# Adjacency attention on one core: three units of seven products in a pass from the sixth pass on, a new order of tiles, the shared product in a unit's second step, left sums in two parts

## What is computed

```python
h = maximum(layernorm(x), 0)                     # x is 4096 x 512
q = h @ Wq.T + bq;  k = key @ Wk.T + bk;  v = value @ Wv.T + bv
scores = (q @ k.T) / 64 * adj                    # adj is 4096 x 4096, of zeros and ones
scores = where(abs(scores) < 1e-5, -1e9, scores)
out = x + (softmax(scores) @ v) @ Wm.T + bm
```

## Time and profile before

| | |
|---|---|
| median of 3 runs | 1549.62 us (1547.48 to 1549.89) |
| the profiled execution | 1546.85 us, its span 1545.0 us |
| TensorE busy | 1522.7 us, 99%, 7064 matmuls |
| VectorE, ScalarE, GpSimd busy | 1061.2, 633.7, 217.9 us |
| DMA, mean share of 16 engines | 73%, 283 MB |

### The profile page before, as it was taken

The page is one execution under the profiler, slowest core; times in us unless marked ns, Lnnn a source line. Parts: engine busy times, 40 slices in busy tenths (PEclk is TensorE's granted clock), DMA queues, the critical chain, the costliest instruction groups (busy, mean ns, idle before and its releaser), DMA issues.

```text
span 1545.0 us, 23780 instructions
## 1 busy us (share of the span) xinstructions
PE 1522.7 (99%) x7064; PEld 700.5 (45%) x7064; DVE 1061.2 (69%) x2191; ACT 633.7 (41%) x1040; POOL 217.9 (14%) x291
## 2 busy tenths in 40 slices
PE   8998999999999999999999999999999999999998
PEld 5543444444444444444444444444444444444444
DVE  5989777766667666666766666676666767676662
ACT  5776433434343333334333334343333434333332
POOL 6164000020020101002010010201001020200100
PEclk9999999999999999999999999999999999999999
DMA  9834786678868687686868768676866868787664
GB/s 346 280 78 98 184 200 154 155 194 217 200 164 205 150 229 173 168 209 157 206 155 231 173 162 210 154 211 163 223 171 162 212 149 216 170 211 174 147 163 109
DMA packets 459508, 283.24 MB, mean 183 GB/s; under 512 B 377411, under 2 KB 385859, under 8 KB 459334
## 3 DMA queue, kind: packets, MB, share of 16 engines
q1 hardware_dynamic: 459456, 282.67, 72.7%
q10 hardware_dynamic: 6, 0.01, 0.0%
HBM read 175.38 MB, written 15.73 MB: 124 GB/s over the span
## 4 chain that ended last, share of the span: by engine, by line
PE 92%; DVE 3%; ACT 2%; DMA 2%; issue 1%; SPq 0%; ACTq 0%; DVEq 0%
PE R L833 15%; PE R L835 15%; PE R L834 15%; PE S L833 11%; PE S L835 11%; PE S L834 11%; PE M L833 3%; PE M L835 3%; PE M L834 3%; PE R L951 1%; PE R L904 1%; DMA pT<-ph 0%; DMA Kbuf<-key_factors 0%; DVE Vbuf L1581 0%; DMA pT<-osb 0%
## 5 line engine op out<-in xcount | busy, mean ns | idle before, releaser
L1293 ACT ACTIVATE drop<-Zbuf 128x512 f32<-128x512 f32 x256 | 161.1, 629 | 687.9 <-DVE cmx L1605 557.7
L833 PE MATMUL R<-Vbuf,pT 128*128 128x512 f16 x1008 | 382.1, 379 | 4.8 <-DMA pT<-ph 2.4
L835 PE MATMUL R<-Vbuf,pT 128*128 128x512 f16 x1008 | 382.0, 379 | 0.0
L834 PE MATMUL R<-Vbuf,pT 128*128 128x512 f16 x1008 | 382.0, 379 | 0.0
L833 PE MATMUL S<-Kbuf,qT 128*128 128x512 f16 x738 | 279.7, 379 | 0.0
L834 PE MATMUL S<-Kbuf,qT 128*128 128x512 f16 x738 | 279.7, 379 | 0.0
L835 PE MATMUL S<-Kbuf,qT 128*128 128x512 f16 x738 | 279.7, 379 | 0.0
L1657 DVE SCALAR_TENSOR_TENSOR Zbuf<-S,rs,adjb 128x512 f32<-128x512 f32 x178 | 133.5, 750 | 210.2 <-PE S L835 199.8
L1605 DVE CUSTOM_DVE_ANT_0 Zbuf<-drop,Zbuf 128x512 f32<-128x512 f32 x256 | 178.2, 696 | 0.0
L833 PEld LDWEIGHTS R<-Vbuf,pT 128*128 128x128 f16 x1008 | 98.6, 98 | 125.8 <-DMA pT<-ph 4.9
L835 PEld LDWEIGHTS R<-Vbuf,pT 128*128 128x128 f16 x1008 | 98.6, 98 | 118.9
(11 more groups left out here) (277 smaller groups left out, 1828.7 us busy)
## 6 DMA issues: line engine op xcount, KB each, us to landing
Kbuf<-key_factors SPq DMA_DIRECT2D x134, 512.0 KB, 4.2
adjb<-in_adj_dram SPq DMA_DIRECT2D x256, 256.0 KB, 2.9
xq<-in_x_dram SPq DMA_DIRECT2D x32, 256.0 KB, 2.8
Kbuf<-in_L_gnn_key_dram SPq DMA_DIRECT2D x8, 1024.0 KB, 13.7
xr<-in_x_dram SPq DMA_DIRECT2D x32, 256.0 KB, 3.0
out_dram<-xr SPq DMA_DIRECT2D x31, 256.0 KB, 4.3
Vbuf<-in_L_gnn_value_dram SPq DMA_DIRECT2D x7, 1024.0 KB, 7.9
key_factors<-early SPq DMA_DIRECT2D x32, 128.0 KB, 2.3
```

The costliest lines, as they stand in the source:

```text
L833: nc.tensor.matmul(ps, lhs[0], rhs[0], start=start, stop=False, skip_group_check=added)
L834: nc.tensor.matmul(ps, lhs[0], rhs[1], start=False, stop=False, skip_group_check=added)
L835: return nc.tensor.matmul(ps, lhs[1], rhs[0], start=False, stop=stop, skip_group_check=added)
L1293: nc.scalar.activation(drop[:, :], tile_of(s.i, s.j), ACT.Abs).then_inc(abs_ready, 1)
```

## The change

From the sixth pass on a third unit is made of tiles 3 and 2, at steps 2 and 3, ahead of the other two; its second half is in steps 9 and 11, so that steps 8 to 12 and 14 all have six score matmuls. The fourth and fifth pass keep two units. The order of tiles is new in all passes after the first, in both halves and for the probabilities. T2 moves from a unit's step 0 to its step 1, ahead of T1, and the sum of it on VectorE with it. The left sums are made in two parts: GpSimd begins in step 0 instead of step 1 and hands over S1 and S2 first, ScalarE copies two halves of 512 columns, and VectorE makes the low half of the first at the end of step 2, of the second in step 3 behind `tile_max`. Four more factors stay in `Kbuf`, in the place of key tiles 2 and 3 (slots -4 to -1); a pass has 13 factor loads in place of 10. The factors' sums are made in the bank `M0`, and 16 more half-pieces are made in steps 3 of the fourth to 2 of the fifth pass. Six passes are now written out. `kept` is renamed `common`.

```diff
-        UNITS = [(5, 4), (7, 6)]
+        UNITS = [(5, 4), (7, 6), (3, 2)]
...
             return Vbuf[:, :].bitcast(fp16)[:, at:at + D]

-        FIRST_ORDER, SECOND_ORDER = [0, 1, 2, 3, 5, 4, 7, 6], [4, 0, 5, 1, 6, 2, 7, 3]
-        SECOND_PROBS = [4, 5, 6, 7, 0, 1, 2, 3]
-        UNIT, NU, MAKE_STEP, FIRST = 4, len(UNITS), 19, 4
+        FIRST_ORDER, SECOND_ORDER = [0, 1, 3, 2, 5, 4, 7, 6], [4, 2, 5, 3, 6, 0, 7, 1]
+        SECOND_PROBS = [3, 2, 5, 4, 7, 6, 0, 1]
+        UNIT, NU, MAKE_STEP, FIRST = 4, len(UNITS), 19, 6
+        TWO_FROM, THREE_FROM = 3, 5
         RING_Q, MIX_Q = (4, 5, 6), 7
+        KEPT_TWO = {(0, "B11"): 0, (0, "T2"): 1, (1, "B11"): 2, (1, "T2"): 3}
+        KEPT_THREE = {(2, "B11"): -4, (2, "T2"): -3, (0, "B21"): -2, (1, "B21"): -1}
+        TURNS_TWO = {4: [(0, "B21"), (1, "B21"), (0, "T3"), (1, "T4")], 5: [(0, "T1"), (1, "T1"), (0, "T4")],
+                     6: [(0, "B22"), (1, "B22"), (1, "T3")]}
+        TURNS_THREE = {4: [(2, "B21"), (0, "T1"), (1, "B22"), (0, "T4"), (1, "T4")], 5: [(2, "T1"), (0, "B22"), (0, "T3"), (2, "T4")],
+                       6: [(2, "B22"), (1, "T1"), (2, "T3"), (1, "T3")]}
...
-        XF = W[0]
+        XF = M0
+        LATE = [W[0], S[0], S[1]]
...
+                if s.three:
+                    if s.j == 3:
+                        sp.wait_ge(kt_stored, 16 * 2 * len(PIECES))
+                        wait(sp, scores_done, s.t)
+                        load_factor((0, "T1"), 4)
+                        wait(sp, unit_mm, 3 * s.before + 3)
+                        load_factor((0, "B22"), 5)
+                    if s.j == 4:
+                        wait(sp, scores_done, s.t)
+                        load_factor((1, "T1"), 6)
+                    if s.j == 5:
+                        wait(sp, unit_mm, 3 * s.before + 6)
+                        load_factor((1, "B22"), 4)
+                    if s.j == 6:
+                        wait(sp, scores_done, s.t)
+                        load_factor((0, "T3"), 5)
+                    if s.j == 7:
+                        wait(sp, unit_mm, 3 * s.before + 9)
+                        load_factor((2, "T3"), 6)
+                    if s.j in (8, 9, 10, 11):
+                        wait(sp, scores_done, s.t)
+                        load_factor(((0, "T4"), (2, "T4"), (1, "T3"), (1, "T4"))[s.j - 8], (4, 5, 6, 4)[s.j - 8])
+                    if s.prefetch and s.j in (12, 13, 15):
+                        wait(sp, scores_done, s.t)
+                        load_factor((2, {12: "T1", 13: "B22", 15: "B21"}[s.j]), {12: 5, 13: 6, 15: 4}[s.j])
...
+                nth = i - TWO_FROM
                 for p, full in enumerate(FULLS):
                     hi, lo = [qT[:, p, h, :, :].rearrange("p s n -> p (s n)") for h in range(2)]
+                    wait(pool, q_in, 16 * (2 * i + p))
+                    wait(pool, p_lo, PASS * (i - 1) + NC - 2)
                     nc.gpsimd.tensor_tensor(full, hi, lo, ALU.add).then_inc(s_steps, 1)
...
-                wait(pool, s_steps, 4 * nth + 2)
+                wait(pool, p_lo, PASS * (i - 1) + NC)
+                wait(pool, s_steps, 3 * nth + 2)
                 nc.gpsimd.tensor_tensor(s1, a21, a22, ALU.add).then_inc(s_steps, 1)
-                nc.gpsimd.tensor_tensor(s3, a11, a21, ALU.subtract)
-                wait(pool, s_steps, 4 * nth + 3)
-                nc.gpsimd.tensor_tensor(s2, s1, a11, ALU.subtract).then_inc(s_steps, 1)
-                wait(pool, s_steps, 4 * nth + 4)
-                nc.gpsimd.tensor_tensor(s4, a12, s2, ALU.subtract).then_inc(s_made, 1)
+                wait(pool, s_steps, 3 * nth + 3)
+                nc.gpsimd.tensor_tensor(s2, s1, a11, ALU.subtract).then_inc(s_made, 1)
+                wait(pool, s_made, 2 * nth + 1)
+                nc.gpsimd.tensor_tensor(s4, a12, s2, ALU.subtract)
+                nc.gpsimd.tensor_tensor(s3, a11, a21, ALU.subtract).then_inc(s_made, 1)
...
-                if s.strassen and s.j == 1:
+                if s.strassen and s.j == 0:
                     row_mixes(s.i)
...
                     elif s.unit == 0:
                         wait(pe, z1_ready, s.t - 1)
-                        pe.wait_ge(kept_in, 16 * 4)
-                        unit_product(S[s.j % 2], qT[:, 0, :, 0:2, :], 2 * s.w, True).then_inc(unit_mm, 1)
-                        pe.wait_ge(kt_lo, 2 * len(PIECES))
-                        wait(pe, s_ready, s.nth + 1)
-                        unit_product(W[0], qS[:, :, 2:4, :], 2 * s.w + 1, True).then_inc(unit_mm, 1)
+                        pe.wait_ge(kept_in, 16 * (8 if s.three else 4))
+                        unit_product(S[s.j % 2], qT[:, 0, :, 0:2, :], factor_at(s, "B11")[0], True).then_inc(unit_mm, 1)
                     elif s.unit == 1:
                         wait(pe, z1_ready, s.t - 1)
-                        wait(pe, kr_in[5], 48 * s.nth + 16 * (s.w + 1))
-                        unit_product(S[s.j % 2], qS[:, :, 0:2, :], 5, True).then_inc(unit_mm, 1)
+                        wait(pe, s_ready, 2 * s.nth + 1)
+                        unit_product(W[0], qS[:, :, 2:4, :], factor_at(s, "T2")[0], True).then_inc(unit_mm, 1)
+                        unit_product(S[s.j % 2], qS[:, :, 0:2, :], landed_factor(s, "T1"), True).then_inc(unit_mm, 1)
...
-                        if s.w == 0:
-                            wait(pe, kr_in[4], 64 * s.nth + 48)
...
+                        wait(pe, z1_ready, s.t - 1)
+                        unit_product(LATE[s.w], qS[:, :, 4:6, :], landed_factor(s, "T3"), True).then_inc(scores_done, 1)
...
                         if s.unit == 0 and m == 1:
-                            wait(pe, kr_in[4], 64 * s.nth + 16 * (s.w + 1))
-                            wait(pe, p1_ready, NU * s.nth + s.w + 1)
-                            unit_product(S[s.j % 2], qT[:, 0, :, 2:4, :], 4, False).then_inc(scores_done, 1)
+                            wait(pe, p1_ready, s.count + 1)
+                            unit_product(S[s.j % 2], qT[:, 0, :, 2:4, :], landed_factor(s, "B21"), False).then_inc(scores_done, 1)
                         if s.unit == 1 and m == CM - 1:
-                            wait(pe, mixed, 2 * NU * s.nth + 2 * s.w + 2)
-                            wait(pe, kr_in[6], 48 * s.nth + 16 * (s.w + 1))
-                            unit_product(S[s.j % 2], qS[:, :, 6:8, :], 6, False).then_inc(scores_done, 1)
+                            wait(pe, mixed, 2 * s.count + 2)
+                            wait(pe, s_ready, 2 * s.nth + 2)
+                            unit_product(S[s.j % 2], qS[:, :, 6:8, :], landed_factor(s, "B22"), False).then_inc(scores_done, 1)
...
                 if s.unit == 0:
-                    wait(act, unit_mm, 6 * s.nth + 3 * s.w + 1)
-                    wait(act, p_lo, PASS * (s.i - 1) + NC + 2 * s.w + 2)
+                    wait(act, unit_mm, 3 * s.count + 1)
+                    wait(act, p_lo, PASS * (s.i - 1) + NC + SECOND_PROBS.index(UNITS[s.w][0]) + 1)
                     nc.scalar.activation(SUM_U[s.w], S[s.j % 2][:, :], ACT.Copy).then_inc(p1_ready, 1)
...
                 if s.strassen and s.j == 2:
-                    act.wait_ge(x_step, chain_before(len(PIECES)))
+                    act.wait_ge(x_step, chain_before(16))
                     wait(act, scores_done, PASS * s.i)
-                    wait(act, s_made, s.nth + 1)
-                    nc.scalar.activation(qS[:, 0, :, :].rearrange("p s n -> p (s n)"), mixes, ACT.Copy).then_inc(s_hi, 1)
+                    for k in range(2):
+                        wait(act, s_made, 2 * s.nth + k + 1)
+                        nc.scalar.activation(qS[:, 0, 4 * k:4 * k + 4, :].rearrange("p s n -> p (s n)"), mixes[:, k * CW:(k + 1) * CW], ACT.Copy)\
+                            .then_inc(s_hi, 1)
...
+            def low_of_mixes(s, k):
+
+                wait(dve, s_hi, 2 * s.nth + k + 1)
+                high, low = [qS[:, h, 4 * k:4 * k + 4, :].rearrange("p s n -> p (s n)") for h in range(2)]
+                nc.vector.tensor_tensor(low, mixes[:, k * CW:(k + 1) * CW], high, ALU.subtract).then_inc(s_ready, 1)
...
-                if s.unit == 0:
-                    wait(dve, p1_ready, NU * s.nth + s.w + 1)
-                    wait(dve, unit_mm, 6 * s.nth + 3 * s.w + 2)
+                if s.unit == 1:
+                    wait(dve, p1_ready, s.count + 1)
+                    wait(dve, unit_mm, 3 * s.count + 2)
                     nc.vector.tensor_tensor(SUM_U[s.w], W[0][:, :], SUM_U[s.w], ALU.add).then_inc(mixed, 1)
-                if s.unit == 1:
-                    wait(dve, unit_mm, 6 * s.nth + 3 * s.w + 3)
+                    wait(dve, unit_mm, 3 * s.count + 3)
                     wait(dve, drop_ready, s.t)
-                    wait(dve, p_lo, PASS * (s.i - 1) + NC + 2 * s.w + 1)
-                    wait(dve, mixed, 2 * NU * s.nth + 2 * s.w + 1)
+                    wait(dve, p_lo, PASS * (s.i - 1) + NC + SECOND_PROBS.index(UNITS[s.w][1]) + 1)
```

(9 more changed lines are left out.)

130 lines of the change are left out of this document (74 added, 56 removed).

## The result

The changed kernel takes 1678.18 us (median of 4 runs, 1672.28 to 1681.32) where the one before takes 1548.62 (median of 4): 1.083 times as long, 95% interval 1.080 to 1.086. The forecast of 1640 had the direction, and its range ended 8 us too low. The profiled execution took 1678.1 us.

The account below looks back on a forecast made before the run. TensorE, 99% busy, was taken as the bound, at 0.2158 us per matmul plus waits. 1546.85 - 14.2 + 11 x (8.3 + 0.8) + 5 = 1637.8, with 2.8 for the runs' median 1640 us; range 1606 to 1670.

Parts of the forecast that it names:

- The matmuls removed: Six fewer matmuls in each of 11 three-unit passes, 66 at 0.2158 us: 14.2 us less.
- wait 1: T2 in step 3 waits for the left sums of its own pass: 3.46 us per pass.
- wait 2: B22 in step 3 waits for T1's sum, `tile_max` and the second low half on VectorE: 0.57 us.
- wait 3: B21 waits for ScalarE's copy in steps 2, 4 and 6: 0.5, 2.5 and 1.3 us.
- the bounds of 7.6 to 8.9: Range for the first half's waits per pass, forecast at 8.3 us, with hand-overs 0.1 us shorter or longer each.
- the 9.1 forecast: Waits per three-unit pass: 8.3 us in the first half plus 0.8 us in the second.
- The third rival: Only part of the waits is paid, since one lets others catch up: 4 to 6 us per pass, 1585 to 1610; 13%.
- the weighing of the clock: No row shows a 3.3 us wait's effect on TensorE's clock; the skill's rule would add time, the sum added none.
- The second rival: TensorE's clock falls to 1.2 GHz in T2's step 3 wait, slowing fifteen matmuls after each: 36 us more, 1676; 12%.
- the term for passes 4 and 5: Two-unit passes with T2 moved, B21 waiting, and the third unit's 16 half-pieces made: +5 us together.
- wait 4: Transposes land late in the shorter steps 8 to 12, nearly all at step 12: 0.8 us per pass, bounds 0 and 2.5.
- The fourth rival: DMA bounds the second half with 13 factor loads; late transposes cost 3 us or more per pass: 1670 or more; 8%.

Follow-up runs that it names:

- experiment 1: Changed kernel with ScalarE's two copies of the left sums ahead of step 2's |z| and VectorE's first low half right behind z; 1625.21 us.
- experiment 3: Changed kernel with ScalarE's copy of B11's bank of step 4 put ahead of the row's output in step 3; 1642.95 us.
- experiment 8: Changed kernel with B21 put six matmuls later in every unit, ahead of the last quarter of the value product; 1656.46 us.
- experiment 2: Changed kernel with 12 extra matmuls of raw operands in step 3 ahead of T2's wait, into a bank that T2 overwrites; 1653.14 us.
- Experiments 4 and 10: Changed kernel, 4: with one factor load moved from step 10 to step 9's end, 1679.24 us; 10: with another second-half tile order alone, 1664.29 us.

## Why the prediction was wrong

**What held.** The matmuls removed (14.2); wait 1, which 3.13 measured and its removal in experiment 1 confirm; wait 2, 0.42 (its own terms add up to 0.51, not 0.57); wait 3 in all three steps, 4.0 for 4.3, in step 4 by the chain on ScalarE that experiment 3 cut, in step 6 with the copy behind VectorE's split, as the trace has it at 982.66 us; the bounds of 7.6 to 8.9 for the three, of which 7.6 was paid. That all waits of a pass add up to the 9.1 forecast is luck: the first half was 0.7 too high and the second 0.7 too low. The third rival (only part of the waits is paid) falls with experiment 1, though experiment 8 shows that B21 and T2 do share step 2.

**The step that failed** is the weighing of the clock: "by the rows alone it stands". The rows showed no wait of 3 us after the start, so they said nothing for or against, and the sum took the silence as a zero. The second rival had the mechanism and nearly the size: 15 matmuls after each wait, 36 us, 1676; measured are some 9 after T2's wait and as many after step 4's in two passes of three, 2.7 us per pass or 30 in all, of which experiment 2 gave 25 back by filling the wait with matmuls. The rule of the Trainium skill that was cited beside it (TensorE: Matmul & The Clock Gate, section HAM oscillation: the clock falls when the engine idles between bursts) agrees with what the trace now shows, 0.50 after 2.97 us of idle time. Two waits as long in experiment 3 had no such fall behind them. Twelve in a hundred was too little for it. The range was too narrow as well: the bounds of the sum's own terms reach 1673 and this rival stood at 1676, but it ended at 1670.

**Mis-sized** was the term for passes 4 and 5: +5, measured 17.9, and nearly all of the difference in the fourth pass, beyond the bound of 12. There B21 waited 7 us in place of 2.6, transposes 6 in place of nothing (both by the distances), and 3.6 are the clock again. I had costed the 16 half-pieces as work (0.384 on ScalarE, sums of 0.7 on VectorE), not as places in a queue: in the trace ScalarE's copy of a half-piece stands ahead of |z| and waits for a store of 4.45 us. That this is the cause is not shown. What this store and what VectorE's sums cost each was not separated: the short stores were no shorter in time, the short sums took 1.5 us of B21's wait but nothing of the time, and moving the work made the pass longer.

**Wrong in kind, and half the size,** was wait 4: 0.8 forecast for transposes, 1.5 measured, most of it a factor load that SP issues late. Experiments 4 and 10 show that a new order of tiles removes it, while an earlier issue only puts a wait for a transpose in its place. The fourth rival (1670 or more by DMA alone) falls: the second half costs 1.5 us per pass, not 3.

**Open**: the 1.7 us that a mended pass still loses, and the 13.5 of the fourth and fifth. Neither bytes, nor one wait by itself, nor the place of the making was their only cause.

## What to carry over

A wait of TensorE can have a second price, the slow matmuls behind it, paid in nearly each repetition; where no row shows a wait of that length, the price is unknown and not zero, and belongs into the range with real weight. Before a product is moved ahead, look at what stands ahead of its operands' last copy on the engine that makes it: here ScalarE was idle for 2.9 us right in front of the |z| that held the copies up. A kernel whose engines are two thirds busy and wait nowhere has its slack in the order; a saving of 1.3 us per pass is not worth an order that uses up the slack of three queues.
